# Layers 2 and 3 of a graph network: gathered columns in two sets of banks, scatter sums behind the gather, node numbers kept on chip

## The reference, cut to what matters

```python
def _L0_gnn_ref(feat, edge_src, edge_dst):          # 10 rounds of the same sum over edges
    for _ in range(10):
        msg = h[edge_src] * norm[edge_src]
        agg = jax.ops.segment_sum(msg, edge_dst, num_segments=n)
        h = 0.9 * (agg * norm) + 0.1 * feat_0
def _L1_gnn_ref(embeds, rows, cols, qTrans, kTrans, vTrans):   # attention over edges
    att = exp(clip((rowEmb @ qTrans) . (colEmb @ kTrans), -10, 10))   # for each of 4 heads
    out = segment_sum(att / (segment_sum(att, rows)[rows] + 1e-08) * (colEmb @ vTrans), rows)
def _L2_gnn_ref(feat, weight, W_self, b_self, W_neigh, b_neigh, src, dst):
    neigh_sum = jax.ops.segment_sum(feat[src] * weight[:, None], dst, num_segments=n)
    return feat @ W_self.T + b_self + (neigh_sum / deg @ W_neigh.T + b_neigh)
def _L3_gnn_ref(weight, ps_w, review_feat, cj, ci, src, dst):
    msg = jax.nn.sigmoid(review_feat @ ps_w.T) * (weight * cj)[src]
    return jax.ops.segment_sum(msg, dst, num_segments=n) * ci

h = jnp.maximum(_layernorm(x), 0.0);  x = x + _L0_gnn_ref(h, src, dst)
h = jnp.maximum(_layernorm(x), 0.0);  x = x + _L1_gnn_ref(h, src, dst, ...)
h = jnp.maximum(_layernorm(x), 0.0);  x = x + _L2_gnn_ref(h, edge_weight, ...)
h = jnp.maximum(_layernorm(x), 0.0);  x = x + _L3_gnn_ref(h, ps_w, edge_attr_64, cj, ci, src, dst)
```

## Time and profile before

| | us |
|---|---|
| median of 3 runs | 1372.91 (1372.68 to 1375.38) |
| the profiled execution | 1385.22 |
| its span, first to last instruction | 1383.5 |

### The profile page before, as it was taken

The page is one execution under the profiler, slowest core; times in us unless marked ns, Lnnn a source line. Parts: engine busy times, 40 slices in busy tenths (PEclk is TensorE's granted clock), DMA queues, the critical chain, the costliest instruction groups (busy, mean ns, idle before and its releaser), DMA issues.

```text
span 1383.5 us, 33061 instructions
## 1 busy us (share of the span) xinstructions
PE 1017.2 (74%) x12016; PEld 759.4 (55%) x12016; DVE 998.4 (72%) x1271; ACT 569.2 (41%) x1383; POOL 611.2 (44%) x445
## 2 busy tenths in 40 slices
PE   4957556775999999999924577686760888647884
PEld 3635446775444444444413576676660777636774
DVE  7894888997455555555546799999986788557885
ACT  1321116665110111101102676776760787407873
POOL 1018888888878878888888890000000000000000
PEclk9978666555999999999966788888875899858997
DMA  7644104553122222222250766765729776307663
GB/s 157 129 99 91 24 2 153 183 175 125 41 62 61 55 62 64 62 59 56 63 124 2 242 224 249 291 227 223 273 94 383 259 261 259 122 21 252 256 262 98
DMA packets 73566, 202.20 MB, mean 146 GB/s; under 512 B 36667, under 2 KB 37467, under 8 KB 73509
## 3 DMA queue, kind: packets, MB, share of 16 engines
q1 hardware_dynamic: 57300, 186.25, 37.2%
q10 hardware_dynamic: 2465, 13.60, 4.3%
q0 software_dynamic: 13744, 1.59, 3.8%
HBM read 155.30 MB, written 45.63 MB: 145 GB/s over the span
## 4 chain that ended last, share of the span: by engine, by line
PE 37%; DVE 25%; issue 15%; DMA 13%; ACT 6%; DVEq 2%; SPq 2%; ACTq 0%; another core or an unknown queue 0%
PE ps L1507 20%; DMA hl_room<-slot_rows 10%; PE ps L1331 4%; PE ps L1307 3%; ACT arena L595 3%; DVE arena L870 2%; DMA hl_room<-in_edge_attr_dram 2%; PE ps L1374 2%; DVE arena L916 2%; PE ps L1468 2%; ACT arena L562 1%; DVE hl_room L1031 1%; PE ps L1361 1%; DVE arena L839 1%; DVE xs_room L1127 1%
## 5 line engine op out<-in xcount | busy, mean ns | idle before, releaser
L522 POOL DMA_INDIRECT w_table<-wpa,slot_i x425 | 606.0, 1426 | 219.5 <-issue 219.5
L1507 PE MATMUL ps<-arena,hl_room 125*128 125x500 f16 (+1 forms) x1750 | 344.5, 353 | 14.2 <-DVEq L1095 9.4
L1307 PE MATMUL ps<-arena 125*128 125x64 f16 (+1 forms) x3900 | 239.7, 213 | 123.9 <-ACT arena L562 64.4
L1307 PEld LDWEIGHTS ps<-arena 125*128 125x128 bf16 x3900 | 180.6, 103 | 136.9 <-ACT arena L562 64.2
L1507 PEld LDWEIGHTS ps<-arena,hl_room 125*128 125x128 f16 x1750 | 155.2, 97 | 176.4 <-DVEq L1094 9.5
L1331 PE MATMUL ps<-arena 128*128 128x128 f16 (+1 forms) x1950 | 170.8, 234 | 21.3 <-DVE arena L848 8.7
L665 ACT ACTIVATE part_room<-ps 128x500 f16<-128x500 f32 (+1 forms) x70 | 38.0, 543 | 322.8 <-PE ps L1507 293.2
L1331 PEld LDWEIGHTS ps<-arena 128*128 128x128 bf16 (+1 forms) x1950 | 144.2, 104 | 39.7 <-issue 14.8
L1103 DVE SCALAR_TENSOR_TENSOR part_room<-ps,part_room 128x500 f16<-128x500 f32 (+1 forms) x70 | 43.6, 622 | 165.0 <-ACT part_room L665 129.3
L827 DVE TENSOR_SCALAR arena<-hl_room,lane 125x3328 bf16<-125x3328 bf16 x100 | 108.7, 1088 | 49.1 <-DMA hl_room<-slot_rows 42.3
L1312 PE MATMUL ps<-arena 125*128 (+1 forms) x1300 | 140.1, 208 | 0.0
(11 more groups left out here) (251 smaller groups left out, 1308.3 us busy)
## 6 DMA issues: line engine op xcount, KB each, us to landing
hl_room<-slot_rows SPq DMA_DIRECT2D x100, 832.0 KB, 6.2
arena<-ohd_table SPq DMA_DIRECT2D x37, 832.0 KB, 4.6
arena<-ohs_table SPq DMA_DIRECT2D x25, 832.0 KB
hl_room<-in_edge_attr_dram ACTq DMA_DIRECT2D x17, 750.0 KB
ohs_table<-xs_room SPq DMA_DIRECT2D x25, 448.0 KB
ohs_table<-xs_room SPq DMA_DIRECT2D x25, 384.0 KB
w_table<-wpa,slot_i POOLq DMA_INDIRECT x425
ohd_table<-hl_room SPq DMA_DIRECT2D x13, 448.0 KB
```

The costliest lines, as they stand in the source:

```text
L522: pool.indirect_dma_start(w_table, bass.IndirectOffsetOnAxis(slot_i[:, u:u + 1], 0), wpa[:, u], None).then_inc(S[f"w_out{g % 2}"], 16)
L1307: last = pe.matmul(ps[:, m % RING, o:o + b - a], slots[:, k * L:(k + 1) * L], rhs, start=(i == 0), stop=(i == 1))
L1507: last = pe.matmul(ps[:, c, 0:w], hl[0:P, u, s, :], adj[:, s, c * CH * P:c * CH * P + w], start=(s == 0), stop=(s == T - 1))
```

## The change

**Layers 2 and 3, PE and banks.** The gather's groups become 8, 8, 8 and 2 columns. Groups 0 to 2 of a tile go to banks 0 to 2 or 3 to 5 by the tile's parity, group 3 goes to columns 128 to 255 of bank 6 or 7, beside the scatter sum (`gathered_at`). A bank is written again when the tile two before has been read. In PE's step the gather of tile s-1 comes first and the scatter sum of tile s-4 after it. The scatter sum has a new wait (`behind`): ACT must have weighted its groups of tile s-2. DVE's and ACT's orders are the same.

**Layers 2 and 3, tables.** Kept on chip are now the rows of node numbers of the 13 even tiles (`kept_rows`). Rows of odd tiles come through one room, and the scatter's matrix is loaded for every tile, into two rooms (`ohd2_words`, one of them `base_room`). Before layer 2, SP loads the row of tile 0, then that of tile 1, then the other 12.

**Layer 1.** Both rows of a tile have two rooms.

**Layer 0.** The halves of layer 1's scatter matrices are made at six of the seven chunks instead of five: 12 for each pair of iterations, at chunks 0 to 4 and 6. The last pair has two left.

```diff
-        GROUPS = {"l1": [2] * (C // 2), "l2": [8, 8, 5, 5], "l3": [8, 8, 5, 5]}
+        GROUPS = {"l1": [2] * (C // 2), "l2": [8, 8, 8, 2], "l3": [8, 8, 8, 2]}
...
+        def gathered_at(m, par, n):
+            if m < 3:
+                return ps[:, 3 * par + m, 0:n * D]
+            return ps[:, RING + par, EXTRA:EXTRA + n * D]
...
-        ROOMS = {"l1": 1, "l2": 2, "l3": 2}
+        ROOMS = {"l1": 2, "l2": 2, "l3": 2}
...
                 def body(d, par, on, pair_no):
-                    if 0 in on:
+                    if 0 in on and p == "l1":
                         for e, tab in enumerate(tables):
-                            room = e if p == "l1" else par
-
-                            sp.wait_ge(S["l1_first" if p == "l1" and e == 0 else p + "_ohT"], d + 1)
-                            sp.dma_start(rowbc[:, room], slot_rows[tab, bass.ds(d * (C * L), C * L)].partition_broadcast(L)
-                                         ).then_inc(S[p + f"_row{room}"], 16)
+                            sp.wait_ge(S["l1_first" if e == 0 else "l1_ohT"], d + 1)
+                            row(rows_l1[e][:, par], tab, d).then_inc(S[f"l1_row{e}{par}"], 16)
+                    if 0 in on and p != "l1" and par:
+                        sp.wait_ge(S[p + "_ohT"], d + 1)
+                        row(rowbc[:, 0], tables[0], d).then_inc(S[p + "_odd_row"], 16)
+                    if p == "l2" and 1 in on and 2 not in on:
+                        for k in range(1, (T + 1) // 2):
+                            row(kept_rows[:, k], tables[0], 2 * k).then_inc(S["kept_rest"], 16)
...
-                    if 2 in on and p != "l1" and par:
+                    if 2 in on and p != "l1":
                         sp.wait_ge(S[p + "_scat"], d - 1)
-                        sp.dma_start(odd_words, ohd_table[bass.ds(d - 2, 1)].rearrange("t p x -> p (t x)")
-                                     ).then_inc(S[p + "_odd_oh"], 16)
+                        sp.dma_start(ohd2_words[par], ohd_table[bass.ds(d - 2, 1)].rearrange("t p x -> p (t x)")
+                                     ).then_inc(S[p + f"_ohd{par}"], 16)
+                if p == "l2":
+                    sp.wait_ge(S["l1_agg"], 1)
+                    row(kept_rows[:, 0], tables[0], 0).then_inc(S["kept_first"], 16)
...
-                        if 1 <= c <= 5:
-                            scatter_one_hots(i * (T // (K0 // 2)), u * 5 + (c - 1))
+                        if c != NCH - 2:
+                            k = u * (NCH - 1) + (c if c < NCH - 2 else c - 1)
+                            if more or k < 2 * T - STAGED * (K0 // 2 - 1):
+                                scatter_one_hots(i * (STAGED // 2), k)
...
+                    if p != "l1" and m == ng - 1 and late:
+                        pe.wait_ge(S[p + "_sums"], t - 1)
...
+                        if p != "l1":
+                            pe.wait_ge(S[p + "_last_rows"], behind * BY_ACT)
...
                 def body(s, par, on, pair_no):
                     c = 0
-                    if 4 in on and p != "l1":
-                        scatter(s - 4, par, 0, C, pair_no - 2)
                     for m, n in enumerate(groups):
                         if 1 in on:
-                            gather(s - 1, 1 - par, m, c, n)
+                            gather(s - 1, 1 - par, m, c, n, 4 in on)
                         if 4 in on and p == "l1" and m == RING - 1:
-                            scatter(s - 4, par, 0, C, pair_no - 2)
+                            scatter(s - 4, par, 0, C)
                         c += n
+                    if 4 in on and p != "l1":
+                        behind = s + 1 if 2 in on else T + 2
+                        scatter(s - 4, par, 0, C, behind)
```

More of the change, by code:

```diff
@@ L235, in graph_net @@
         ohd = [ohd_words[:, g].rearrange("p (a r b) -> p a r b", a=CP, b=2) for g in range(2)]
+        more_rows = cv([L, 2, C * L], BF16)
         assert cv.at <= edge_end
+        rows_l1 = [rowbc, more_rows]
         cv = Carver()
@@ L375, in load_rows, with row @@
                 if p == "l1":
-                    sp.sem_inc(S["l1_first"], 1)
+                    sp.sem_inc(S["l1_first"], free)
+                def row(room, tab, d):
+                    return sp.dma_start(room, slot_rows[tab, bass.ds(d * (C * L), C * L)].partition_broadcast(L))
                 def body(d, par, on, pair_no):
-                    if 0 in on:
+                    if 0 in on and p == "l1":
                         for e, tab in enumerate(tables):
-                            room = e if p == "l1" else par
-                            sp.wait_ge(S["l1_first" if p == "l1" and e == 0 else p + "_ohT"], d + 1)
-                            sp.dma_start(rowbc[:, room], slot_rows[tab, bass.ds(d * (C * L), C * L)].partition_broadcast(L)
-                                         ).then_inc(S[p + f"_row{room}"], 16)
+                            sp.wait_ge(S["l1_first" if e == 0 else "l1_ohT"], d + 1)
[6 more added lines that the diff above has]
+                            row(kept_rows[:, k], tables[0], 2 * k).then_inc(S["kept_rest"], 16)
                     if 2 in on and p == "l1":
@@ L453, in _ @@
                 one_hots_kept(sp)
-                sp.wait_ge(S["l1_agg"], 1)
-                for k in range((T + 1) // 2):
-                    sp.dma_start(kept_words[:, k], ohd_table[2 * k]).then_inc(S["kept_in"], 16)
                 load_rows("l2", (0,))
@@ L823, in ohT_of @@
                     if p == "l1":
-                        vec.wait_ge(S[f"l1_row{e}"], s * 16 + 16)
-                    else:
-                        vec.wait_ge(S[p + f"_row{par}"], s * 8 + (16 - 8 * par))
-                    done = vec.tensor_scalar(ohT[:, par, e] if p == "l1" else ohT2[:, par], rowbc[0:P, e if p == "l1" else par], lane[0:P, :], None, ALU.is_equal)
+                        vec.wait_ge(S[f"l1_row{e}{par}"], s * 8 + (16 - 8 * par))
+                        room, to = rows_l1[e][0:P, par], ohT[:, par, e]
+                    elif par:
+                        vec.wait_ge(S[p + "_odd_row"], s * 8 + 8)
+                        room, to = rowbc[0:P, 0], ohT2[:, par]
+                    else:
+                        if p == "l2" and type(s) is int and s in (0, 2):
+                            vec.wait_ge(S["kept_rest" if s else "kept_first"], 16 * ((T - 1) // 2 if s else 1))
+                        room, to = kept_rows[0:P, bass.ds(pair_no, 1)].rearrange("p k n -> p (k n)"), ohT2[:, par]
+                    done = vec.tensor_scalar(to, room, lane[0:P, :], None, ALU.is_equal)
                     done.then_inc(S[p + "_ohT" if e == ends - 1 else "l1_first"], 1)
@@ L1284, in edge_layer, with gather @@
                 pe.wait_ge(S["parts_ready"], n_parts)
-                if p == "l2":
-                    pe.wait_ge(S["kept_in"], 16 * ((T + 1) // 2))
-                def gather(t, par, m, c, n):
+                def gather(t, par, m, c, n, late):
                     if m == 0:
```

47 lines of the change are left out of this document (20 added, 27 removed).

## The result

| | before | after |
|---|---|---|
| median, us | 1372.8 (1372.14 to 1375.38) | 1430.88 (1426.21 to 1439.84, 4 runs) |
| the profiled execution, its span | 1385.22, 1383.5 | 1429.94, 1428.2 |
| mean granted clock of PE | 0.828 | 0.828 |

The changed kernel is slower: 1.042 times the kernel before (95% interval 1.039 to 1.044), 58 us. The forecast was 1424, between 1381 and 1436. The sum came out; one of its steps did not, and most of what follows is about it.

The account below looks back on a forecast made before the run. PE was taken to bound layer 0, a DVE-ACT chain layers 2 and 3. Savings of -26.7 us and +78 for a new loop through SP gave +51 on the median 1372.9: 1424 us, range 1381 to 1436.

Parts of the forecast that it names:

- Layer 0: Layer 0 and its end: waits for last features and `x` go, last-iteration halves fall away; -17.0 us in all.
- the last features: Layer 0: PE's nine waits for an iteration's last new features go entirely; -4.3 us.
- the wait for `x`: After layer 0: the store finishes an iteration earlier, so DVE's 10.72 us wait before L1151 goes; -10.7 us.
- Layer 1: Layer 1: second rooms don't help requests queued on SP behind the scatter-sum wait; -0.4 us, for the start only.
- Start of layer 2: Start of layer 2: tile 0's row loads first, and tile 2's one-hot waits for the fourteenth transfer; -6.5 us.
- Steady pace: Layers 2 and 3: DVE-ACT chain stays at 4.75 us a step; two bank sets win at most 1.4 a layer, -2.8.
- Register-addressed sums: Layers 2 and 3: sums addressed by register drop from 3.42 to 1.62 us, but off the chain; 0 gained.
- The loop through SP: Layers 2 and 3: one-hot, gather, sum, SP, next odd row takes 13.4 us per two tiles, not 9.5; +78 us.
- the landing: Loop in layers 2 and 3: from SP's issue of a row behind a matrix to its use, 6.06 us.
- The new wait for ACT's reads is not the last: Layers 2 and 3: ACT's weighting ends 0.4 us into the next step, before the late gather, so this wait doesn't matter.
- The rival of a warm loop: Layers 2 and 3: PE's clock stays up, loop 11.5 us, total 1387; warm or mixed (1383 to 1411) had chance 0.25.
- The rival of rows in time: Layers 2 and 3: odd rows land early enough, steps stay 4.75 us and all savings remain; 1346 us, chance 0.14.

Follow-up runs that it names:

- e11: The kernel before with only layer 0's part of the change, the scatter-matrix halves at six of seven chunks: 0.987 of the kernel before.
- e12: The kernel before with only two rooms for each row of layer 1, SP's order as it was: 1.003 of the kernel before.
- e6: The changed kernel with PE's part undone in layers 2 and 3 and layer 1's rows requested before the scatter-sum waits: 0.975 of the kernel before.
- e10: The changed kernel with PE's part undone and rows requested before the scatter-sum waits, both in layers 2 and 3: 0.984 of the kernel before.
- e4: The kernel before with only PE's part of the change (bank sets, groups, sum behind gather, new waits), old tables: 1.064 of the kernel before.
- e2: The changed kernel with each tile's fourth group in the other of banks 6 and 7, sum not waiting for ACT's same-step weighting: 1.050 of before.
- e1: The changed kernel with SP requesting odd tiles' rows ahead of its waits for scatter sums in layers 2 and 3: 1.035 of the kernel before.
- e7: The changed kernel with both the edits of e1 and e2, sum still behind the gather: 0.989 of the kernel before.

## Why the prediction was right, and where not

*Layer 0.* Forecast -17.0. e11 has -17.7 by its runs, whose interval is wide, and the traces have -14.3 and -14.6. The single terms: the last features 4.3 forecast, 4.8 found (PE's first to last chunk, 355.9 and 351.1); the wait for `x` 10.7 forecast, 10.6 gone and 2.6 of it given back at L1183, which the forecast did not have.

*Layer 1.* Forecast -0.4, since the requests stand behind a wait on SP that the rooms don't change. Right: e12 gained nothing, and e6, which moves the requests, gained the layer 17 us.

*Start of layer 2.* Forecast -6.5, found -5.0. The mis-sized term is the 14 transfers, 32.9 us for 31.1.

*Steady pace, -2.8.* The size was about right (209.2 us in e10 for 213.0 before) and the cause wrong. I put the ragged steps down to PE's room in the banks. e10, with the old banks and early rows, has none of them.

*Register-addressed sums, 0.* Right only for the old order. In the new one the same sum is in loop B, and e4, which keeps the register, took 11.6 us more in the two layers than the change.

*The loop through SP, +78.* Found +69.9 in the two layers together (22 steps of each), +75.9 with what lies around them. One-hot to one-hot was 12.5 and 13.3 us on average, with a forecast of 13.4 for a cold PE and 11.5 for a warm one. The terms of it, by the means over nine periods a layer: the landing, taken as 6.06, was 5.97 and 6.17; SP's part, taken as 0.89, was 1.04 and 1.30; gather and sum, taken as 5.14 for a cold PE, were 4.24 and 4.55. So the loop was at the lower level only in part. Alone, in e2, it takes 146.0 and 155.2 us a layer, 13.3 and 14.1 a pair; there the late gather is slow in every one of the periods measured (2.95 us at 1332.34 and 1345.35).

The 2.0 us that the prediction has from the Trainium skill ("DMA: Bandwidth & Descriptors", section on the anatomy of one DMA) stand there for transfers that the general engine issues, while these are SP's. By that estimate matrix and row would be in 6.4 us after the matrix's issue; they took 6.8 and 7.1 on average. Nothing in the sum rests on it.

*The step that failed* is "The new wait for ACT's reads is not the last". I compared the end of ACT's weighting with the late gather ahead of the sum, and for the even step that holds. I did not ask who waits for the sum besides SP. ACT does: its high half needs the sum's room, so the wait closes a second loop, which runs through the very engine that is waited for. It takes 5.58 us a step with PE's clock at the upper level and 6.91 where the clock is at the lower one during the sum, 136.8 and 137.1 us a layer in e1. The two loops are of nearly the same length, so either hides the other, and the total came out right with one of them missing from the account. That is luck in the sum, and it would have misled the repair: the prediction would have asked for early rows alone, which bring 0.7% (the intervals of e1 and the change touch).

*The rival of a warm loop* (1387) didn't hold: the granted clock of layers 2 and 3 is 0.91 and 0.88 in the changed kernel, 0.99 and 0.98 before. The rival of rows in time (1346) named early rows as what decides it; with early rows the time was 1.035 of before.

What stays open: why rows take longer to land in e2 than in the change, what decides in e1 whether a stretch of steps has the slow sum, and whether the two sets of banks cost something small.

## What to carry to other kernels

When a step is moved behind others on one engine, list everyone who waits for its result or for the room it frees, not only the one that looks late, and follow each back to where the moved step now starts; two loops of similar length hide each other, so that taking away either shows nothing. Ask for a transfer ahead of waits that it doesn't need: on a queue that issues in program order its place was worth 17 us in layer 1, while a second room behind the same wait was worth nothing.

## What the runs showed of the hardware

The sum of 26 matmuls took 1.62 us or, after 1.5 us of idle in a loop that repeats it, 2.96 in step after step, while the gather behind it ran near full speed within the same step: the granted clock was 0.50 over the one and 0.98 over the other (e1). After 1.5 us of idle the same sum was also seen at full speed for many steps in the same layer (5.58 us each, granted clock 1.00), and in e7 PE stood 1.5 us ahead of every gather with a granted clock of 1.00. So the length of the idle time alone, in these rows, doesn't tell which level follows.
